# Attention over 16 images: the order of a batch's seven score products, and where the statistics and the input of the next batch stand

## The chip, the cores and the metric

The kernel runs on one core of one Trainium2 chip. The metric is the device time of one execution in microseconds (us), the median over several executions. A second, profiled execution gives the trace that the rows below are taken from; times in it are counted from the first instruction.

The engines are named as in the profile: PE is TensorE (matmuls), PEld its weight loads, DVE is VectorE, ACT is ScalarE, POOL is GpSimd, and SP is the engine that only issues transfers (DMAs). Each engine works through its own list of instructions in order. Where an instruction has to wait for another engine, everything behind it on the same engine waits as well.

## The reference

For each of 16 images `x` (512 channels, 32x32 = 1024 positions):

```python
h = group_norm(x, gn_w, gn_b)            # 32 groups of 16 channels
q, k, v = split(qkv_w @ h + qkv_b)       # three 512x512 products
attn = softmax((q^T k) / sqrt(512))      # 1024 x 1024
o = out_w @ (v attn^T) + out_b
return x + o
```

The softmax runs over the keys. Everything is float32, and the result must be float32-accurate.

## The kernel before

**Arithmetic.** The weights are multiplied together once, so that a batch has four steps on PE. T: `t = G h` with G the product of the weights of q and k. S: the scores, `t^T h`, 1024 keys by 1024 queries. V: `v = h^T U` with U the product of the weights of v and of the output. A: the output, `v` times the exponentials. Every float32 operand is kept as a rounded upper part (`_hi`, fp32r) and the rest (`_lo`), and each product is three matmuls, hi-hi, hi-lo and lo-hi (lines 459 to 461). ACT writes the upper parts; DVE writes the rests.

**Seven products in place of eight.** T, S and V (but for batch 0's T and V) are done as block products of Strassen's kind: seven products named A11, A12, S1, S2, S3, A22 and S4, each of a block of the one matrix, or a sum of blocks, with a block of h or a sum of blocks of h (`t1` to `t4`, written by `h_combined` and split by `h_combined_rest`, line 1289). The list `PRODUCTS` gives their order in the score step; T and V have lists of their own, which name the products.

**The score step on PE** (`score_products`). Each product has four units of six matmuls, one for each of four PSUM banks. A11 is opened in banks 0 to 3. ACT copies it to banks 4 to 7 (`copy_first`, line 869, semaphore `s_p1`), where A12 is added to it; ACT copies the sum to SBUF with the key bias (`copy_scores`, line 881): that is the first quarter of the scores (`s_c11`). In banks 0 to 3 the products S2, S3 and A22 are added one after the other, and between two of them ACT copies each bank out: after S2 (`s_p2`), after S3 (`s_p3`) and after A22 (`s_c21`, a quarter of the scores). S3's unit i waits for `s_p2` of bank i, and A22's unit i for `s_p3` of bank i. S1 is opened in banks 4 to 7 as soon as A12's sum has been copied out; DVE adds it to the copy made after S3 (`add_scores`, line 1438; `s_c22`). S4 is added on top of S1 once `s_c22` is there, and DVE adds that sum to the copy made after S2 (`s_c12`). The order before is A11, A12, S1, S2, S3, A22, S4.

**Half 0 and half 1.** Queries 0 to 511 are half 0, queries 512 to 1023 are half 1. Half 0's scores are `c11` and `c21`, half 1's are `c22` and `c12`. `max_step` (line 1450) keeps a running maximum of each half, POOL spreads it over the partitions (`max_all`, line 1165), `subtract_max` (line 1457) takes it off, and ACT does the exponential (line 900) and the upper part (line 915).

**The splits of t.** `t_sum_rest` (line 1431; line 1379 in batch 0) writes the rests of S1, S2, S3 and S4 in this order; between those of S2 and of S3 stand three `max_step`s of `c11`. Each counts `s_tlo` up. ACT, before its four copies after S2, waits until `s_tlo` is complete: `act.wait_ge(s_tlo, splits(b + 1))`.

**The statistics of the next batch.** x of batch b+1 is loaded into `xs`, the same tile that held x of batch b. ACT first adds the output bias to `xs` (`shift_input`, line 888), SP stores it to `out` (line 425), and then loads the next x (line 429). DVE then takes the statistics (`stats_part`, eight instructions, line 1230). `group_stats` on SP writes them to DRAM (line 370), waits until they have landed and reads them back with one group to a partition (line 378). After that DVE joins them (`group_variance`, lines 1562 and 1564), ACT takes the root (`group_std_part`, line 894) and does a small exponential behind it (line 895), so that the exponential's table is loaded again, and DVE forms the inverse (`group_root`), which SP spreads over the channels. ACT's instructions of a batch stand in one list, in which the four copies after S2 come before the four after S3, those before the four after A22, and those before `group_std_part`.

**The next T step.** T's third product, S2, needs `t2`, the second `h_combined_rest` of the batch. DVE does the first one (`t1`) before the four `scale_output`s (line 1547) of the output's half 1, and the others behind them. POOL loads the blocks of U that don't stay in SBUF (`load_u`, lines 1150 and 1152), four transfers of 1.5 MB together, once the score step's S2 is done.

Of the kernel before, what the change touches and what calls it, by code (L numbers as in the profile page):

```python
# [45 lines left out]
PRODUCTS = [(A11, "b11"), (A12, "b21"), (S1, "t1"), (S2, "t2"), (S3, "t3"), (A22, "t4"), (S4, "b22")]  # L46
P_A11, P_A12, P_S1, P_S2, P_S3, P_A22, P_S4 = range(7)
# [62 lines left out]
def attention_kernel(nc, x, wq, wk, wv, wo_t, cols, block_avg, out):  # L110
# [5 lines left out]
    with ctx:  # L116
# [228 lines left out]
        def _(sp):  # L345
# [69 lines left out]

            def store_u_s2():
# [4 lines left out]
            for b in range(B):  # L421
                for k in range(CT):
                    if b + 1 < B:
                        sp.wait_ge(s_shifted, b * CT + k + 1)
                        sp.dma_start(out_v[b, :, k, :], xs[:, k, :]).then_inc(s_sent[k], DMA)
                if b + 1 < B:
                    for k in range(CT):
                        sp.wait_ge(s_sent[k], (b + 1) * DMA)
                        sp.dma_start(xs[:, k, :], x_v[b + 1, :, k, :]).then_inc(s_x[k], DMA)
                    group_stats(b + 1)  # L430
# [315 lines left out]
        def _(act):  # L746
# [231 lines left out]
            for b in range(B):  # L978
# [29 lines left out]
                for k in range(CT):  # L1008
# [3 lines left out]
                    shift_input(b, k)  # L1012

                act.wait_ge(s_tlo, splits(b + 1))
                for i in range(CT):
                    copy_scores(b, P_S2, i, i, 8 + i, s_p2)
                if b == 0:
# [9 lines left out]
                if b + 1 < B:  # L1027
                    group_std_part(b + 1)
                if b == 0:
# [49 lines left out]
                if b + 1 < B:  # L1079
# [9 lines left out]
                    for c in range(CT):  # L1089
# [3 lines left out]
                        h_combined_part(b + 1, c)  # L1093

# [110 lines left out]
        def _(dve):  # L1205
# [403 lines left out]
            for b in range(B):  # L1609
# [57 lines left out]
                if more:  # L1667
                    for q in range(CT * NB):
                        stats_part(b + 1, q)
                if b == 0:  # L1670
                    for n, a in enumerate((S1, S2, S3, S4)):
                        g_sum_rest(a, n)
                if b == 1:
                    for n, a in enumerate((S1, S2, S3, S4)):
                        u_sum_rest(a, n)
                for i in range(CT):
# [3 lines left out]
                for i in range(CT):  # L1680
                    max_step(b, 0, CT + i, CT + i, s_c21, b * 4 + i + 1)
                if more:
                    group_variance(b + 1)
                for i in range(CT):
                    add_scores(b, P_S4, i, 8 + i, s_p2, s_c12)
                    max_step(b, 1, CT + i, i, s_c12, b * 4 + i + 1)

                for q in range(CT):
                    subtract_max(b, 0, q)
                if more:  # L1690
                    group_root(b + 1)
                    group_spread(b + 1)
                if b == 0:
# [6 lines left out]
                    if more:  # L1700
                        affine_pair(b + 1)
# [6 lines left out]
                else:  # L1708
# [16 lines left out]
                    if more:  # L1725
                        affine_pair(b + 1)
# [19 lines left out]
                if more:  # L1746
                    for k in range(CT):
                        key_dot(b + 1, k)
                    h_combined_rest(b + 1, 0)
                for c in range(CT if more else CT - 1):  # L1750
# [33 lines left out]
```

## Time and profile before

| | |
|---|---|
| three runs | 1984.97, 1984.98 and 1986.65 us, median 1984.98 |
| the profiled execution | 1984.35 us |
| its span, first to last instruction | 1982.6 us |
| PE busy | 1973.3 us |
| DVE busy | 1667.9 us (84% of the span) |
| ACT busy | 1123.0 us (57%) |
| POOL busy | 447.9 us (23%) |

The chain that ended last is made of PE for 91%. Busy times of an engine are those in which it had an instruction in hand; matmuls overlap, so the mean duration of one (389 ns for 512 columns) is more than the distance from one start to the next. The profiled execution's own time is 1.75 us more than its span, and 0.63 us under the median of the three runs.

In a timeline a row is: start, duration, engine, line, operation, what it writes and reads, how many of them; in brackets the idle time of the engine before it and what ended it.

### The profile page before, as it was taken

How to read it: one execution, taken by the hardware profiler on the slowest of the kernel's cores; microseconds unless marked ns; L12 is line 12 of the kernel's file. 1: busy time of each engine (PE TensorE's matmuls, PEld its weight loads, DVE VectorE, ACT ScalarE, POOL GpSimd, SP SyncE). 2: the span in 40 equal slices, each digit the busy share in tenths (PEclk: the TensorE clock that was granted, in tenths of full speed). 3: DMA queues.
4: the chain of work that ended last, by engine and by line, in shares of the span. 5: the costliest groups of instructions: out<-in, count | busy, mean ns of one | idle time of the engine just before them, and what ended most of it. 6: DMA issues, size and time to landing. Idle time of an engine off the chain costs nothing.

```text
span 1982.6 us, 26069 instructions
## 1 busy us (share of the span) xinstructions
PE 1973.3 (100%) x9895; PEld 1681.2 (85%) x9895; DVE 1667.9 (84%) x2010; ACT 1123.0 (57%) x1431; POOL 447.9 (23%) x306
## 2 busy tenths in 40 slices
PE   9999999999999999999999999999999999999999
PEld 7888878888888888888888888888888888888888
DVE  8897987969889798797988979788797988969866
ACT  6564636646465564645746466563664646556461
POOL 1112140121412213131131401214022141221311
PEclk9999999999999999999999999999999999999999
DMA  6305143051431604325033240424305143150411
GB/s 177 129 7 130 59 74 119 6 139 49 75 118 16 167 12 75 119 41 153 6 73 116 58 136 6 113 76 74 120 7 143 45 75 118 19 171 4 75 33 54
DMA packets 102636, 157.89 MB, mean 80 GB/s; under 512 B 49376, under 2 KB 51264, under 8 KB 102512
## 3 DMA queue, kind: packets, MB, share of 16 engines
q0 software_dynamic: 31264, 73.15, 17.0%
q1 hardware_dynamic: 71248, 83.08, 13.7%
q8 instruction: 79, 1.29, 0.3%
q14 instruction: 45, 0.37, 0.1%
HBM read 85.57 MB, written 68.26 MB: 78 GB/s over the span
## 4 chain that ended last, share of the span: by engine, by line
PE 91%; DVE 4%; DMA 2%; ACT 1%; issue 1%; POOL 1%; SPq 0%; DVEq 0%; POOLq 0%; ACTq 0%
PE ring L459 30%; PE ring L461 30%; PE ring L460 30%; DMA stage<-stage 1%; DVE r_lo L1289 1%; DMA out<-all_max 0%; DVE stage L1457 0%; POOL stage L1170 0%; DVE h_lo L1264 0%; DVE stage L1524 0%; ACT stage L761 0%; POOL out L1179 0%; DMA stage<-wq 0%; DVE stage L1373 0%; ACT stage L774 0%
## 5 line engine op out<-in xcount | busy, mean ns | idle before, releaser
L459 PE MATMUL ring<-r_hi 128*128 128x512 f32 (+1 forms) x1724 | 656.6, 381 | 0.2 <-DVE r_lo L1477 0.2
L460 PE MATMUL ring<-r_lo,r_hi 128*128 128x512 f32 (+1 forms) x1724 | 656.4, 381 | 0.0
L461 PE MATMUL ring<-r_hi,r_lo 128*128 128x512 f32 (+1 forms) x1724 | 656.2, 381 | 0.0
L459 PEld LDWEIGHTS ring<-r_hi 128*128 128x128 f32 x1724 | 324.2, 188 | 62.2 <-DVE r_lo L1477 0.7
L461 PEld LDWEIGHTS ring<-r_hi,r_lo 128*128 128x128 f32 x1724 | 324.2, 188 | 62.0
L460 PEld LDWEIGHTS ring<-r_lo,r_hi 128*128 128x128 f32 x1724 | 324.2, 188 | 61.4
L881 ACT ACTIVATE stage<-ring,keybias 128x512 f32<-128x512 f32 x256 | 175.2, 685 | 164.3 <-PE ring L461 161.6
L1170 POOL PARTITION_ALL_REDUCE stage<-stage x32 | 127.3, 3977 | 465.8 <-DVE stage L1530 465.8
L854 ACT ACTIVATE stage<-ring,by_tile 128x512 f32<-128x512 f32 x120 | 82.5, 688 | 250.7 <-PE ring L461 250.7
L1462 DVE TENSOR_TENSOR r_lo<-stage,r_hi 128x1024 fp32r<-128x1024 f32 x128 | 182.2, 1453 | 0.0
L1450 DVE TENSOR_TENSOR run_max<-run_max,stage 128x512 f32<-128x512 f32 x192 | 132.0, 694 | 54.1 <-ACT stage L881 49.3
L459 PE MATMUL ring<-h_hi,r_hi 128*128 128x512 f32 x444 | 172.8, 389 | 0.2 <-DVE r_lo L1379 0.2
L461 PE MATMUL ring<-h_hi,r_lo 128*128 128x512 f32 x444 | 172.7, 389 | 0.0
L460 PE MATMUL ring<-h_lo,r_hi 128*128 128x512 f32 x444 | 172.7, 389 | 0.0
L1457 DVE TENSOR_TENSOR stage<-stage,all_max 128x1024 f32<-128x1024 f32 x128 | 151.8, 1228 | 0.0
L900 ACT ACTIVATE stage<-stage 128x1024 f32<-128x1024 f32 x128 | 134.5, 1051 | 18.7 <-DVE stage L1457 18.7
L915 ACT ACTIVATE r_hi<-stage 128x1024 fp32r<-128x1024 f32 x128 | 135.8, 1061 | 2.9 <-PE ring L461 0.3
L1165 POOL PARTITION_ALL_REDUCE all_max<-run_max x32 | 57.9, 1810 | 304.6 <-DVE run_max L1450 160.2
L761 ACT ACTIVATE stage<-xs,by_tile 128x1024 f32<-128x1024 f32 x62 | 76.5, 1233 | 83.3 <-DMA sum_row<-stage 82.6
L1230 DVE BATCH_NORM_STATS2 stats<-xs 128x6 f32<-128x512 f32 x128 | 80.7, 684 | 47.3 <-DMA xs<-x_in 47.1
L1150 POOL DMA_DIRECT2D r_hi<-u_dram x15 | 8.5, 570 | 461.3 <-PE ring L461 461.3
L767 ACT ACTIVATE r_hi<-stage 128x1024 fp32r<-128x1024 f32 x64 | 68.0, 1063 | 76.1 <-DVE stage L1279 71.5
(199 smaller groups left out, 3979.2 us busy)
## 6 DMA issues: line engine op xcount, KB each, us to landing
xs<-x_in SPq DMA_DIRECT2D x64, 512.0 KB, 5.7
out<-xs SPq DMA_DIRECT2D x60, 512.0 KB, 2.7
out<-run_max POOLq DMA_DIRECT2D x60, 256.0 KB, 5.6
inv<-inv_row SPq DMA_DIRECT2D x32, 256.0 KB, 4.5
out<-spare POOLq DMA_DIRECT2D x30, 256.0 KB, 7.6
out<-all_max POOLq DMA_DIRECT2D x30, 256.0 KB, 5.0
r_hi<-g_dram POOLq DMA_DIRECT2D x15, 512.0 KB, 6.2
r_lo<-g_dram POOLq DMA_DIRECT2D x15, 512.0 KB, 5.5
```

Source lines behind the costliest of these rows:

```text
L459: nc.tensor.matmul(ps_out, st_hi, m_hi, start=first, stop=False, skip_group_check=goes_on)
L460: nc.tensor.matmul(ps_out, st_hi, m_lo, start=False, stop=False, skip_group_check=goes_on)
L461: return nc.tensor.matmul(ps_out, st_lo, m_hi, start=False, stop=last, skip_group_check=goes_on)
L854: nc.scalar.activation(stage[:, to + kk, :], ring[:, T_BANK[p] + kk, :], ACT.Identity, bias=t_bias[:, i:i + 1]).then_inc(done, 1)
L881: nc.scalar.activation(stage[:, to, :], ring[:, bank + i, :], ACT.Identity, bias=keybias[:, m:m + 1]).then_inc(done, 1)
L900: nc.scalar.activation(here, here, ACT.Exp, scale=SCALE).then_inc(s_exp, 1)
L915: nc.scalar.activation(p_pair(r_hi, b, nb, q), stage[:, 8 * nb + 2 * q:8 * nb + 2 * q + 2, :], ACT.Copy).then_inc(s_phi, 1)
L1170: nc.gpsimd.partition_all_reduce(stage[:, 8 * nb + 1, :], stage[:, 8 * nb, :], P, bass.bass_isa.ReduceOp.add).then_inc(s_allsum, 1)
L1230: nc.vector.bn_stats(stats[:, k, half, :], xs[:, k, half * HALF:(half + 1) * HALF]).then_inc(s_stats, 1)
L1450: nc.vector.tensor_tensor(run_max[nb][:, :], first, stage[:, 8 * nb + m, :], ALU.max).then_inc(s_rmax[nb], 1)
L1457: nc.vector.tensor_tensor(here, here, all_max[:, :].rearrange("p (o n) -> p o n", o=1).to_broadcast([P, 2, HALF]), ALU.subtract).then_inc( ...
L1462: nc.vector.tensor_tensor(p_pair(r_lo, b, nb, q), stage[:, 8 * nb + 2 * q:8 * nb + 2 * q + 2, :], p_pair(r_hi, b, nb, q).bitcast(FP32), AL ...
```

## The change

- `PRODUCTS` becomes A11, A12, S2, S3, A22, S1, S4. T's and V's orders stay, since their lists go by name.
- POOL's `load_u` waits for the score step's S2 by its number in the list, so it starts when the third product is done and not the fourth.
- ACT: from batch 1 on `group_std_part(b + 1)` stands right behind the four copies after S2, ahead of the four after S3 (in batch 0 it stays behind those after A22). `shift_input` stays between the copies of `c11` in batch 0 alone; for the later batches it stands at the end of the batch before, behind `h_combined_part`.
- SP: the stores of the shifted input, and the loads of the next, are a function, `change_input`. They stand at the same place in SP's list.
- DVE: from batch 1 on `group_variance`, `group_root` and `group_spread` stand right behind the eight `stats_part`s (in batch 1 with the splits of U's sums between them). Then come half 0's four last `max_step`s, then S1's four `add_scores` with their maxima, then S4's, with half 0's four `subtract_max`es between them in pairs. The second `h_combined_rest` moves ahead of the four `scale_output`s of half 1.

```diff
--- before.py
+++ after.py
@@ -43,8 +43,8 @@
 
 
 A22, S1, A11, S2, S3, A12, S4 = range(7)
-PRODUCTS = [(A11, "b11"), (A12, "b21"), (S1, "t1"), (S2, "t2"), (S3, "t3"), (A22, "t4"), (S4, "b22")]
-P_A11, P_A12, P_S1, P_S2, P_S3, P_A22, P_S4 = range(7)
+PRODUCTS = [(A11, "b11"), (A12, "b21"), (S2, "t2"), (S3, "t3"), (A22, "t4"), (S1, "t1"), (S4, "b22")]
+P_A11, P_A12, P_S2, P_S3, P_A22, P_S1, P_S4 = range(7)
 
 
 T_PRODUCTS = [P_A11, P_S1, P_S2, P_A12, P_S3, P_A22, P_S4]
@@ -413,20 +413,23 @@
                 for at, name in ((0, "a11"), (1, "a12")):
                     sp.dma_start(by_rows(u_dram[side, :, at, :]), u_raw(t, name).bitcast(FP32)).then_inc(s_u_out, DMA)
 
+            def change_input(b):
+
+                for k in range(CT):
+                    sp.wait_ge(s_shifted, b * CT + k + 1)
+                    sp.dma_start(out_v[b, :, k, :], xs[:, k, :]).then_inc(s_sent[k], DMA)
+                for k in range(CT):
+                    sp.wait_ge(s_sent[k], (b + 1) * DMA)
+                    sp.dma_start(xs[:, k, :], x_v[b + 1, :, k, :]).then_inc(s_x[k], DMA)
+
             def store_u_s2():
                 for n, (side, t) in enumerate(((0, r_hi), (1, r_lo))):
                     sp.wait_ge((s_uhi, s_ulo)[n], 2)
                     sp.dma_start(u_dram[side, :, 2, :], t[:, u_home(1, S2), :].bitcast(FP32)).then_inc(s_us2_out, DMA)
 
             for b in range(B):
-                for k in range(CT):
-                    if b + 1 < B:
-                        sp.wait_ge(s_shifted, b * CT + k + 1)
-                        sp.dma_start(out_v[b, :, k, :], xs[:, k, :]).then_inc(s_sent[k], DMA)
                 if b + 1 < B:
-                    for k in range(CT):
-                        sp.wait_ge(s_sent[k], (b + 1) * DMA)
-                        sp.dma_start(xs[:, k, :], x_v[b + 1, :, k, :]).then_inc(s_x[k], DMA)
+                    change_input(b)
                     group_stats(b + 1)
                 if b == 1:
                     store_u_s2()
@@ -1009,11 +1012,14 @@
                     if k == 0:
                         act.wait_ge(s_bias_out, (b + 1) * DMA)
                     copy_scores(b, P_A12, k, k, k, s_c11, CT)
-                    shift_input(b, k)
+                    if b == 0:
+                        shift_input(b, k)
 
                 act.wait_ge(s_tlo, splits(b + 1))
                 for i in range(CT):
                     copy_scores(b, P_S2, i, i, 8 + i, s_p2)
+                if 0 < b < B - 1:
+                    group_std_part(b + 1)
                 if b == 0:
                     for n, (a, count) in enumerate(((S1, 5), (S2, 6), (S3, 7), (S4, 8))):
                         g_sum_part(a, n, count)
@@ -1024,9 +1030,8 @@
                     copy_scores(b, P_S3, i, CT + i, 12 + i, s_p3)
                 for i in range(CT):
                     copy_scores(b, P_A22, i, CT + i, CT + i, s_c21)
-                if b + 1 < B:
+                if b == 0:
                     group_std_part(b + 1)
-                if b == 0:
                     exponential(b, 0, 0)
                     p_part(b, 0, 0)
                     exponential(b, 0, 1)
@@ -1091,6 +1096,8 @@
 
                             act.wait_ge(s_unit, unit(b, "A") + CT)
                         h_combined_part(b + 1, c)
+                    for k in range(CT):
+                        shift_input(b + 1, k)
 
         @block.gpsimd
         def _(pool):
@@ -1667,38 +1674,44 @@
                 if more:
                     for q in range(CT * NB):
                         stats_part(b + 1, q)
+                if b > 0 and more:
+                    group_variance(b + 1)
                 if b == 0:
                     for n, a in enumerate((S1, S2, S3, S4)):
                         g_sum_rest(a, n)
                 if b == 1:
                     for n, a in enumerate((S1, S2, S3, S4)):
                         u_sum_rest(a, n)
+                if b > 0 and more:
+                    group_root(b + 1)
+                    group_spread(b + 1)
+                for i in range(CT):
+                    max_step(b, 0, CT + i, CT + i, s_c21, b * 4 + i + 1)
+                if b == 0:
+                    group_variance(b + 1)
                 for i in range(CT):
                     add_scores(b, P_S1, i, 12 + i, s_p3, s_c22)
                     if i > 0:
                         max_step(b, 1, i, CT + i, s_c22, b * 4 + i + 1)
                 for i in range(CT):
-                    max_step(b, 0, CT + i, CT + i, s_c21, b * 4 + i + 1)
-                if more:
-                    group_variance(b + 1)
-                for i in range(CT):
+                    if i % 2 == 0:
+                        subtract_max(b, 0, i)
+                        subtract_max(b, 0, i + 1)
                     add_scores(b, P_S4, i, 8 + i, s_p2, s_c12)
                     max_step(b, 1, CT + i, i, s_c12, b * 4 + i + 1)
-
-                for q in range(CT):
-                    subtract_max(b, 0, q)
-                if more:
+                if b > 0 and more:
+                    affine_pair(b + 1)
+
+                if b == 0:
                     group_root(b + 1)
                     group_spread(b + 1)
-                if b == 0:
                     for q in range(CT):
                         p_rest(b, 0, q)
                         first_v_rest(q)
                     first_v_rest(4)
                     subtract_max(b, 1, 0)
                     subtract_max(b, 1, 1)
-                    if more:
-                        affine_pair(b + 1)
+                    affine_pair(b + 1)
                     first_v_rest(5)
                     sum_tree(b, 0)
                     first_v_rest(6)
@@ -1722,8 +1735,6 @@
                     subtract_max(b, 1, 0)
                     add_v12(b, 1)
                     subtract_max(b, 1, 1)
-                    if more:
-                        affine_pair(b + 1)
                     v12_rest(b, 0)
                     v12_rest(b, 1)
                     subtract_max(b, 1, 2)
@@ -1747,6 +1758,7 @@
                     for k in range(CT):
                         key_dot(b + 1, k)
                     h_combined_rest(b + 1, 0)
+                    h_combined_rest(b + 1, 1)
                 for c in range(CT if more else CT - 1):
                     scale_output(b, 1, c)
                     if not more:
@@ -1755,7 +1767,7 @@
                     last_scale(0)
                     last_scale(1)
                 if more:
-                    for c in range(1, CT):
+                    for c in range(2, CT):
                         h_combined_rest(b + 1, c)
```

## Rows read from the trace of the kernel before

**Rows 1.** The page, part 1: busy time, share of the span, instructions.

```profile
PE 1973.3 (100%) x9895; PEld 1681.2 (85%) x9895; DVE 1667.9 (84%) x2010; ACT 1123.0 (57%) x1431; POOL 447.9 (23%) x306
```

**Rows 2.** PE's waits: line, waited for, us in total, times, longest.

```profile
PE ring L459 <- DVE r_lo L1289: 3.0, 2, 2.0
```

**Rows 3.** Start of batch 2's T step: timelines of DVE and PE; a window with PEclk.

```profile
285.80 5.24 DVE L1289 TENSOR_TENSOR r_lo<-stage,r_hi 128x1024 fp32r<-128x1024 f32 x3
...
288.82 0.50 PE L459 MATMUL ring<-r_hi,g_hi 128*128 128x512 f32 x1 [1.98 <-DVE r_lo L1289]
...
290.10:293.40 3.30, 3.30 (x9) 2.61 (x8) 0.94 (x1) 0.72 (x2) 1.78 (x2) 0.50 0.92 86
```

**Rows 4.** Timeline of PE, score step of batch 5: starts of products 1, 3, 5.

```profile
666.93 0.39 PE L459 MATMUL ring<-h_hi,r_hi 128*128 128x512 f32 x1
...
677.81 0.39 PE L459 MATMUL ring<-r_hi 128*128 128x512 f32 x1
...
688.69 0.39 PE L459 MATMUL ring<-r_hi 128*128 128x512 f32 x1
```

**Rows 5.** Timeline of ACT, score step of batch 5.

```profile
684.89 0.69 ACT L881 ACTIVATE stage<-ring,keybias 128x512 f32<-128x512 f32 x1 [3.04 <-PE ring L461]
...
700.53 1.28 ACT L894 ACT_TABLE_LOAD   x1
702.37 0.20 ACT L894 ACTIVATE by_group<-by_group 32x1 f32<-32x1 f32 x1 [0.55 <-DVE by_group L1564]
...
703.88 0.20 ACT L895 ACTIVATE by_group<-by_tile 32x1 f32<-32x1 f32 x1
```

**Rows 6.** Timeline of DVE, score step of batch 5.

```profile
680.84 0.69 DVE L1450 TENSOR_TENSOR run_max<-run_max,stage 128x512 f32<-128x512 f32 x1 [0.92 <-ACT stage L881]
681.45 2.36 DVE L1431 TENSOR_TENSOR r_lo<-stage,r_hi 128x1024 fp32r<-128x1024 f32 x2
686.77 5.13 DVE L1230 BATCH_NORM_STATS2 stats<-xs 128x6 f32<-128x512 f32 x8 [2.97 <-DMA xs<-x_in]
...
701.16 1.00 DVE L1562 BATCH_NORM_AGGREGATE by_group<-inv 32x2 f32<-32x192 f32 x1
702.19 0.14 DVE L1564 TENSOR_SCALAR by_group<-by_group 32x1 f32<-32x1 f32 x1
```

**Rows 7.** Timelines of SP and POOL, batch 5; then lines 370 and 378, 15 each.

```profile
691.94 0.38 SPq L370 DMA_DIRECT2D stats_d<-stats  x1
697.39 0.32 SPq L378 DMA_DIRECT2D inv<-stats_d  x1
...
689.17 0.57 POOL L1150 DMA_DIRECT2D r_hi<-u_dram  x1 [30.61 <-PE ring L461]
...
DMA to landing us min/median/max: 2.2/4.5/5.5
...
DMA to landing us min/median/max: 1.5/1.7/2.8
```

**Rows 8.** Timeline of PE, the first matmuls of all, and six like them later.

```profile
1.45 4.02 PE L504 MATMUL ring<-spare 128*128 128x512 bf16 x9 [1.45 <-DVE spare L1206]
...
17.05 1.47 PE L504 MATMUL ring<-spare 128*128 128x512 bf16 x6
```

**Rows 9.** Timeline of DVE, batch 1: U's sums and the statistics.

```profile
195.20 2.50 DVE L1506 TENSOR_TENSOR stage<-u_hi,u_lo 128x512 f32<-128x512 f32 x4
...
200.40 4.84 DVE L1230 BATCH_NORM_STATS2 stats<-xs 128x6 f32<-128x512 f32 x8
```

**Rows 10.** Timelines of PE and DVE, score step of batch 0.

```profile
72.21 0.39 PE L459 MATMUL ring<-r_hi 128*128 128x512 f32 x1
...
71.47 1.29 DVE L1379 TENSOR_TENSOR r_lo<-stage,r_hi 128x512 fp32r<-128x512 f32 x2
...
77.39 0.69 DVE L1395 TENSOR_TENSOR stage<-stage,spare 128x512 f32<-128x512 f32 x1
...
84.55 0.69 DVE L1399 TENSOR_TENSOR r_lo<-stage,r_hi 128x512 fp32r<-128x512 f32 x1
```

## The prediction, made before the changed kernel was run

> **What bounds the kernel now.** The page first: PE is busy in 1973.3 of 1982.6 us, no other engine over 84% [rows 1]. So only what makes PE wait can change the time, and nearly nothing is left to be won: the reader should take from this that a gain can be a few us, while a new wait of PE counts in full. Then PE's waits: the only ones of size are for line 1289, `h_combined_rest`, 3.0 us in two [rows 2]. The timeline of DVE and PE shows why: the second `h_combined_rest` stands behind the four `scale_output`s and starts at 285.80, and PE, which needs `t2`, starts again at 288.82 after 1.98 us of idleness. From 290.1 to 293.4 PE then runs at a granted clock of 0.50, 1.2 GHz in place of 2.4 [rows 3]. Last the score step of batch 5, which stands for batches 2 to 14: I need who hands what to whom, and when. PE starts the step at 666.93 and spends 10.88 us on two products, so 5.44 on one and 1.36 on a unit; it does not wait [rows 4]. What follows counts from 666.93 as S+0.
>
> **The second `h_combined_rest`, moved up.** It then ends about 1.2 us after the first and before `t2` is wanted; the four scales behind it slip by 1.2 us, and PE's S1 of the T step, which needs the first two, comes 2.7 us into that step. So the waits of rows 2 go (3.0), the stretch at half clock too (3.3 us at 0.50, 1.65 lost) [rows 3], and a few tenths of restarts: -5.0.
>
> **The input shifted and loaded early.** ACT's four shifts leave the score step and go where ACT idles before the T step; the x transfers land during T. DVE's 2.97 us of idleness for x goes [rows 6], but DVE is not the bound, so by itself 0. It moves one thing: the last maximum of `c11` waited for ACT, which was held up by the shifts. The copy can start 0.28 us after PE's unit, as it does at 684.89, 0.28 after a unit that ended at 683.25 + 1.36 [rows 4, 5]. A12 ends at 677.81, so the copy runs from 678.09 to 678.78 and the maximum starts at 678.81 and not at 680.84 [rows 4, 6]. The rests behind it move by the same 2.03: S4's ends at 681.78 (S+14.85).
>
> **The new order and the copies after S2.** S3 is now due at S+16.32. Its first unit needs the first copy after S2, and ACT makes it only when the rest of S4 is there: S+14.85 + 0.69 = S+15.54. It is 0.8 us in time, from batch 1 on: 0. If that margin is gone, PE waits here and the row will name ACT.
>
> **`group_std_part` ahead of the copies after S3: the large term.** A22 is now due at S+21.76 (688.69) [rows 4], and its first unit needs the first copy after S3. ACT makes that copy only when it is through with `group_std_part`, which waits for `group_variance` on DVE, which waits for a round trip through DRAM, which starts when all eight statistics are done; and these still stand behind S4's rest. Step by step:
> - statistics: DVE is free at 681.78. Eight took 4.84 us where x was there [rows 9], so they end at 686.6. That x is there early helps no more than that, since DVE's list holds them back.
> - the round trip: out, landed, back, landed. The medians are 4.5 and 1.7 us [rows 7], so 6.2. The loads of U lie beside it in the trace: they began 2.8 us before the store (689.17, 691.94) [rows 7]. `load_u` now starts a product earlier, at about 683.7, and the store at 686.6: 2.9 us, the same company, so I take the medians. Back at 692.8.
> - `group_variance`: from 701.16 to 702.33, 1.17 us [rows 6]. 694.0.
> - ACT: root, table load, small exponential, from 702.33 to 704.08, 1.75 us [rows 5] (the table load ahead of the root runs before the wait, at 700.53, and is hidden). 695.7.
> - the copy: 0.69 [rows 5]. 696.4, and PE starts A22 at about 696.5.
>
> Due 688.69, started 696.5: PE idles 7.8 us. Queued behind the waiting `group_std_part` are all of ACT's copies; who waits for them is PE, and behind PE every other engine. A restart costs 0.1 (0.50 for the first matmul [rows 3] in place of 0.39 [rows 4]). After the stall the clock will be down, since 1.98 us of idleness brought it down [rows 3]. The two ends for that: 1.65 us as there, and what the start of the program shows, when PE had done nothing before: nine matmuls took 4.02 us, where at full clock six take 1.47, so nine 2.1, and the two products behind them ran at the lower level as well; with these some 5.3 us at 1.2 GHz, 2.6 lost [rows 8]. An idleness of 7.8 us is nearer to the second: 2.6. A batch then costs 7.8 + 0.1 + 2.6 = 10.5, and 13 batches (2 to 14; the last has no next one) 136.5.
>
> A rule of the skill bears on the round trip. The Trainium skill (DMA: Bandwidth & Descriptors, Anatomy of one DMA) puts a fixed 2.0 us on each transfer, most of it the receipt of the write; two small transfers would be 4.0 us and the sum 2106. The trace has 4.5 and 1.7, and agrees with the rule only at its low end (2.2, 1.5) [rows 7].
>
> **Batch 1** has U's sums between S4's rest and the statistics: 5.2 us (195.20 to 200.40) [rows 9]. Its u loads are over by then, so I take the shortest round trip, 3.7 [rows 7]. S+14.85 + 5.2 + 4.84 + 3.7 + 1.17 + 1.75 = S+31.5; then ACT has four upper parts of U's sums before the copy (put at 2.5, as DVE's four [rows 9]) and 0.69: S+34.7. PE idles 12.9; with 0.1 and 2.6 that is 15.6.
>
> **Batch 0** keeps the old place of `group_std_part`, but not the old order. S3 is due at 72.21, where the fourth product starts now; S4's rest ends at 71.47 + 1.29, the copy 0.69 later, at 73.5 [rows 10]: 1.3. A22's first unit waits for ACT, which first splits G's sums: the last sum is there at 78.1 [rows 10], plus two instructions of at most 0.69 gives 79.4, due 79.05: 0.35. S4's first unit needs `c22`, now behind four maxima (0.69 and a hand-over, 0.8 each), `group_variance` and one addition; the copies of `c21` can't start before 85.24 [rows 10], so 85.9 + 3.2 + 1.2 + 0.7 = 91.0, due 90.4: 0.6. With restarts 2.6 in all.
>
> **Half 0's maxima first, the subtractions in pairs.** In the S4 product DVE now has eight short instructions and four subtractions of 1.2 us, 10 us against PE's 5.44, so `c12` comes late; but V asks for it only at its fifth product, 11 us into V. Covered: 0. `group_root` and `group_spread` leave the V step, and DVE gets slack there that PE can't use: 0.
>
> **The sum.** Against the profiled execution: 1984.35 + 136.5 + 15.6 + 2.6 - 5.0 = 2134.1. The median of the runs stands 0.6 above that execution, so 2135.
>
> **The ends.** Shortest round trip, 3.7, and 1.65 for the clock: 5.3 + 0.1 + 1.65 = 7.05 a batch, 91.7 for 13, batch 1 14.7, in all 2089. Longest round trip, 8.3 (5.5 + 2.8) [rows 7]: 9.9 + 0.1 + 2.6 = 12.6, 164 for 13, batch 1 20, and half clock in batch 0 too (1.65), with only 3 won back: 2170.
>
> **Rivals.**
> 1. *The wait never reaches PE* (not slower). Its place is `group_std_part` on ACT; its price is nothing if the variance is there by S+19.3 (21.76 less 0.69 and 1.75), which with 6.2 and 1.17 before it needs the statistics done by S+11.9. For it: x lands early, and DVE has idle gaps in just that stretch (0.92 us and more before each maximum) [rows 6]. Against it: the statistics stand behind the rests in DVE's list, which end at S+14.85, and nothing takes them forward. It would give 1984.98 - 5.0 + 2.6 = 1982.6, within 0.2%, or a little less if batch 0 loses nothing. 6%.
> 2. *The short round trip.* If the earlier loads of U leave the two small transfers alone, they take 3.7, a batch 8.0, and the time is 2102. For it: batch 1 and the minima of rows 7; against it: the same 2.8 us between the loads and the store as before. The skill's fixed cost, cited above, says nearly the same. 11%.
> 3. *The clock stays down.* If after such a stall PE stayed at 1.2 GHz to the end of the step, the 16.3 us left of it would cost 16.3 and not 2.6: 14 x 13.7 more, 2327. Rows 3 and 8 speak against it: the clock came back after 3.3 and 5.3 us of work. 3%.
>
> My forecast has the other 80%. That the change does less than it says I can't see: PE's first unit of A22 waits for `s_p3` whatever the order.
>
> **How the numbers follow.** About 0.2%, 4 us, is what a measurement of this kernel can tell from no change. Range 2089 to 2170: the forecast with both its ends, and rival 2. Rival 1 lies within 0.2% or just over it; I give 4% to no change and 2% to faster; the rest, 94%, is slower.
>
> **What would show each step.** In PE's waits a new row: `ring L459 <- ACT stage L881` (or what stands before it), 14 long ones of 6 to 10 us, batch 1's about 13. On ACT an idle time of 6 us or more before the root (line 894), ended by DVE's line 1564, and on DVE one before line 1562, ended by the DMA `inv<-stats_d`. PEclk at 0.5 in a stretch after each. No waits for line 1289. Line 1230 without idleness for x. In batch 0 three waits of 0.3 to 1.4 us. Wrong would be: a PE without idle stretches at A22 in batches 2 to 14; a `group_variance` that ends before S+19.3; or stalls at another product, S3 or S4, in the later batches.

## The result, and the profile after

The changed kernel takes 2129.43 us (median of 4 runs, 2128.04 to 2129.98), the kernel before 1985.74 us on the same chip: a ratio of 1.0724, 95% interval 1.0708 to 1.074. It is 144 us slower; the prediction said 2135, 2089 to 2170. The profiled execution has a span of 2128.2 us, 145.6 more than before.

From the page after, part 1, the answer to [rows 1], and from PE's waits, the answer to [rows 2]:

```profile
PE 2003.4 (94%) x9894; PEld 1701.0 (80%) x9895; DVE 1668.5 (78%) x2010; ACT 1114.6 (52%) x1431; POOL 448.5 (21%) x306
...
PE ring L462 <- ACT stage L884: 118.8, 15, 13.1
```

The reader is to see two things. DVE, ACT and POOL are busy for as long as before, within 9 us, with as many instructions: no work was added. PE's share of the span has fallen from 100% to 94%, though its busy time is 30 us longer: the matmuls behind each stall run at the lower clock, as shown below. And one row of waits holds 118.8 of the 145.6 us: line 462 is the hi-hi matmul, line 884 the copy of the scores out of PSUM. The row for `h_combined_rest` is gone.

Batch 5 after, timelines of PE (the first matmul of A22), ACT, DVE, SP and POOL; the score step starts at 711.02, the S+0 of the prediction. They answer to [rows 4 to 7]:

```profile
741.37 0.77 PE L462 MATMUL ring<-r_hi 128*128 128x512 f32 x1 [8.43 <-ACT stage L884]
...
725.88 2.42 ACT L884 ACTIVATE stage<-ring,keybias 128x512 f32<-128x512 f32 x4 [3.03 <-DVE r_lo L1438]
728.32 1.28 ACT L897 ACT_TABLE_LOAD   x1
738.93 0.20 ACT L897 ACTIVATE by_group<-by_group 32x1 f32<-32x1 f32 x1 [9.33 <-DVE by_group L1571]
739.15 1.28 ACT L898 ACT_TABLE_LOAD   x1
740.45 0.20 ACT L898 ACTIVATE by_group<-by_tile 32x1 f32<-32x1 f32 x1
740.56 2.37 ACT L884 ACTIVATE stage<-ring,keybias 128x512 f32<-128x512 f32 x4
...
723.49 2.35 DVE L1438 TENSOR_TENSOR r_lo<-stage,r_hi 128x1024 fp32r<-128x1024 f32 x2
725.76 4.84 DVE L1237 BATCH_NORM_STATS2 stats<-xs 128x6 f32<-128x512 f32 x8
737.72 1.01 DVE L1569 BATCH_NORM_AGGREGATE by_group<-inv 32x2 f32<-32x192 f32 x1 [7.12 <-DMA inv<-stats_d]
...
730.62 0.38 SPq L370 DMA_DIRECT2D stats_d<-stats  x1
735.81 0.33 SPq L378 DMA_DIRECT2D inv<-stats_d  x1
...
727.82 0.57 POOL L1157 DMA_DIRECT2D r_hi<-u_dram  x1 [24.73 <-PE ring L464]
```

Read from the bottom up, this is the chain. The loads of U start at 727.82. The statistics end at 730.60, SP stores them at once, and the store takes until 735.8; the read back takes until 737.7. DVE sits idle for 7.12 us, ACT for 9.33 us with the table for the root already loaded, and behind this wait in ACT's list stand the copies after S3, for which PE waits 8.43 us. The two transfers, 15 each, with the time to landing (lines 370 and 378, the same two rows as in [rows 7]):

```profile
DMA to landing us min/median/max: 2.6/4.8/5.5
...
DMA to landing us min/median/max: 1.5/1.7/1.9
```

The clock after a stall, windows of batch 4 (PE idle, then working at the low clock, then at the full one) and of batch 5; the last three numbers are PEclk, DMA share, GB/s:

```profile
605.00:609.00 4.00, 0.00 (x0) 0.00 (x0) 1.99 (x8) 2.25 (x5) 0.00 (x0) 0.50 0.01 2
609.20:614.80 5.60, 5.60 (x13) 4.39 (x14) 0.69 (x1) 2.29 (x5) 0.00 (x0) 0.50 0.06 4
615.00:620.00 5.00, 5.00 (x24) 4.13 (x23) 2.72 (x4) 1.78 (x3) 0.72 (x1) 1.00 0.01 2
...
737.90:744.50 6.60, 3.13 (x8) 2.50 (x9) 1.81 (x8) 4.10 (x8) 0.00 (x0) 0.50 0.05 1
```

The clock is down to 1.2 GHz while PE is idle, and PE then works at it for 5.7 us in batch 4, 13 matmuls in 5.6 us where 24 fit in 5.0 at 2.4 GHz, and for 3.3 us in batch 5.

### The profile page after: what moved, and what is told of

Same layout as the page of the kernel before. It is cut to its first block, busy times and chain, and to the rows that moved or that the text cites. A ratio compares the mean times of both kernels' runs of the same rounds, so it can differ in the third digit from the quotient of the medians.

```text
span 2128.2 us, 26068 instructions
## 1 busy us (share of the span) xinstructions
PE 2003.4 (94%) x9894; PEld 1701.0 (80%) x9895; DVE 1668.5 (78%) x2010; ACT 1114.6 (52%) x1431; POOL 448.5 (21%) x306
## 4 chain that ended last, share of the span: by engine, by line
PE 86%; DVE 7%; DMA 4%; ACT 2%; issue 1%; ACTq 0%; DVEq 0%
PE ring L462 28%; PE ring L463 28%; PE ring L464 28%; DVE stats L1237 3%; DMA stats_d<-stats 3%; DVE r_lo L1438 1%; DMA inv<-stats_d 1%; ACT stage L884 1%; ACT L898 1%; DVE by_group L1569 1%; DVE run_max L1457 1%; PE ring L485 0%; PE ring L478 0%; PE ring L487 0%; PE ring L507 0%
## 5 line engine op out<-in xcount | busy, mean ns | idle before, releaser
L462 PE MATMUL ring<-r_hi 128*128 128x512 f32 (+1 forms) x1724 | 670.8, 389 | 118.9 <-ACT stage L884 118.8
L463 PE MATMUL ring<-r_lo,r_hi 128*128 128x512 f32 (+1 forms) x1724 | 667.7, 387 | 0.0
L464 PE MATMUL ring<-r_hi,r_lo 128*128 128x512 f32 (+1 forms) x1724 | 666.6, 387 | 0.0
L462 PEld LDWEIGHTS ring<-r_hi 128*128 128x128 f32 x1724 | 331.9, 193 | 188.8 <-issue 123.5
L464 PEld LDWEIGHTS ring<-r_hi,r_lo 128*128 128x128 f32 x1724 | 330.9, 192 | 65.0
L463 PEld LDWEIGHTS ring<-r_lo,r_hi 128*128 128x128 f32 x1724 | 331.9, 192 | 63.2
L884 ACT ACTIVATE stage<-ring,keybias 128x512 f32<-128x512 f32 x256 | 162.9, 681 | 131.0 <-PE ring L464 81.1
L1413 DVE TENSOR_TENSOR stage<-stage,ring 128x512 f32<-128x512 f32 x90 | 60.6, 686 | 79.0 <-PE ring L464 68.8
L935 ACT ACTIVATE ring<-ring 128x512 f32<-128x512 f32 x30 | 17.5, 582 | 186.3 <-PE ring L464 186.3
```

The lines of the kernel that those rows point to most:

```text
L462: nc.tensor.matmul(ps_out, st_hi, m_hi, start=first, stop=False, skip_group_check=goes_on)
L463: nc.tensor.matmul(ps_out, st_hi, m_lo, start=False, stop=False, skip_group_check=goes_on)
L464: return nc.tensor.matmul(ps_out, st_lo, m_hi, start=False, stop=last, skip_group_check=goes_on)
L884: nc.scalar.activation(stage[:, to, :], ring[:, bank + i, :], ACT.Identity, bias=keybias[:, m:m + 1]).then_inc(done, 1)
```

## The experiments

**The place of `group_std_part`, taken back on ACT alone.** From the changed kernel:

```diff
-                if 0 < b < B - 1:
-                    group_std_part(b + 1)
...
-                if b == 0:
+                if b + 1 < B:
                     group_std_part(b + 1)
```

> The changed kernel with one edit: group_std_part goes back behind ACT's four copies after A22. Theory (the copies after S3 wait behind group_std_part for the statistics' round trip): the 14 long waits of PE at A22 (8.2 us each) go. But DVE keeps group_root ahead of half 0's last maxima, and it now waits for ACT's root, which comes after the last copy after A22, at S+29.7 (S is the start of the score step). Then 2.0 us of group_root and group_spread, four maxima 2.9, one addition 0.7: c22 at S+35.2, where S4 is due at S+32.64. So PE waits 2.6 us at S4 in 14 batches, with restart and half clock some 4.5 each: 1980 + 63 = 2043 us. Rival (the new order itself, or the early x, costs PE its time, not the place of group_std_part): the long waits stay at A22, about 2129.

Measured: 2014.69 us, ratio 1.0156 (1.0135 to 1.0176). The long waits at A22 are gone, so the rival falls. In their place stand 1.58 us at S4 in each of batches 2 to 14, and 8.3 in batch 1. DVE, batch 2, and PE:

```profile
342.77 0.15 DVE L1576 RECIPROCAL by_group<-by_group 32x1 f32<-32x1 f32 x1 [2.35 <-ACT by_group L897]
342.95 0.21 DVE L1578 SCALAR_TENSOR_TENSOR by_group<-by_group 32x1 f32<-32x1 f32 x1
...
343.63 3.08 DVE L1456 TENSOR_TENSOR run_max<-run_max,stage 128x512 f32<-128x512 f32 x4
346.63 1.28 DVE L1444 TENSOR_TENSOR stage<-stage,ring 128x512 f32<-128x512 f32 x2
...
347.45 0.47 PE L462 MATMUL ring<-h_hi,r_hi 128*128 128x512 f32 x1 [1.58 <-DVE stage L1444]
```

The mechanism is as expected: root on ACT, `group_root`, four maxima, one addition, PE. The size was not: 2015 us, where I had 2043. `group_root` and `group_spread` took 0.9 us (342.77 to 343.7) and not 2.0, and 1.58 us of idleness did not bring the clock down in any of the 13 batches, so a batch lost 1.8 us and not 4.5. Batch 1 lost 10.6 us, far more than I had allowed. ACT's timeline of batch 1 shows why:

```profile
214.01 2.42 ACT L884 ACTIVATE stage<-ring,keybias 128x512 f32<-128x512 f32 x4 [9.20 <-DVE u_lo L1524]
```

These are the copies after A22. They wait for the splits of U's sums, which stand behind the variance on DVE, and the root stands behind the copies.

**The place of the statistics' steps, put into the kernel before.** The order of the products, x and t2 stay:

```diff
                     copy_scores(b, P_S2, i, i, 8 + i, s_p2)
+                if 0 < b < B - 1:
+                    group_std_part(b + 1)
...
+                if b > 0 and more:
+                    group_variance(b + 1)
...
```

(both are taken from their old places)

> The kernel before with one part of the change: from batch 1 on group_variance stands right behind the statistics and group_std_part ahead of the copies after S3; the order of the products, x and t2 stay as before. Theory: the place of group_std_part alone is enough. The statistics end at S+25.2 (they wait for x), 6.3 for the round trip, 1.2, 1.75 and the copy 0.7 give S+35.3, where A22 is due at S+27.2 in the old order: 8.1 idle, with restart and clock 10.4, 13 times 135, batch 1 about 12: 2132 us. Rival (the stall needs the new order, in which A22 comes a product earlier): no long waits, 1985 us.

Measured: 2124.05 us, ratio 1.0707 (1.0686 to 1.0728). PE's waits:

```profile
PE ring L459 <- ACT stage L881: 112.4, 14, 9.4
```

Fourteen waits of 7.5 to 9.4 us in the kernel before, from this edit alone. The sum had said 2132, 8 us too much; the waits of 13 batches are 7.9 us in the mean, as forecast within 0.2, and part of the rest is that the stretch at half clock for `t2` did not come in this execution. The move is enough, and the new order is not needed for it: A22 comes a product earlier in the changed kernel, but so do the statistics, and the two cancel.

**The loads of U held back.** In the changed kernel:

```diff
                 pool.wait_ge(s_unit, unit(b, "S") + 4 * P_S2 + 4)
+                if 1 < b < B - 1:
+                    pool.wait_ge(s_gstep, b * GSTEP + 2)
```

> The changed kernel, with POOL's loads of U held back in batches 2 to 14 until group_variance is done. Theory (the first half of the round trip is long, 4.9 us, because 1.5 MB of U move beside it): the store lands in 2.3 to 2.7 us as in batches 0 and 1, PE's idle time at A22 falls from 8.2 to about 5.8 us, 13 x 2.4 = 31 less: 2098 us. Rival (the transfer is slow for itself, or by something else such as the number of its small packets): it still takes 4.9 us, 2129 us. V needs U only 13 us later, so no new wait at V in either case.

Measured: 2099.82 us, ratio 1.0585 (1.0564 to 1.0606), 30 us less than the changed kernel. Time to landing of the store of the statistics, and PE's waits:

```profile
DMA to landing us min/median/max: 2.1/2.4/3.0
...
PE ring L462 <- ACT stage L884: 86.4, 15, 12.6
```

The store fell from 4.8 to 2.4 us and PE's waits by 32.4 us, 2.5 in each of the 13 batches. The 24 KB of the statistics are slow because 1.5 MB of U are on their way. What is left, 2.4 + 1.7, is the round trip alone. The Trainium skill (DMA: Bandwidth & Descriptors, Anatomy of one DMA) gives a fixed 2.0 us for a transfer that GpSimd issues; these two go out from SP, and each half is close to it all the same. The same page (Latency and other measured facts) puts HBM's latency at 0.2 us on average and at 2 us at high load; the 2.4 us that the loads of U add point the same way, but no run here separates that latency from the queues.

**The statistics moved forward.** The changed kernel, with the condition of the first rival made true:

```diff
                     t_sum_rest(b, S2)
+                    if more:
+                        for q in range(CT * NB):
+                            stats_part(b + 1, q)
+                    t_sum_rest(b, S3)
+                    t_sum_rest(b, S4)
                     for i in range(1, CT):
                         max_step(b, 0, i, i, s_c11, b * 4 + i + 1)
-                    t_sum_rest(b, S3)
-                    t_sum_rest(b, S4)
+                    if more:
+                        group_variance(b + 1)
```

> The changed kernel with the statistics of the next x moved forward on DVE, ahead of the rests of S3 and S4, and the three c11 maxima and group_variance behind those. This makes the condition of the prediction's first rival true: x is there at about S+7.5, the statistics run from S+8.5 to S+13.3, before the loads of U start, so the round trip is 4.3, the variance is done at S+18.9 and ACT has made the first copy after S3 at S+21.5, due S+21.76. Theory: the long waits of batches 2 to 14 vanish or shrink below 0.5 us, and a wait of 0.1 to 0.3 us at S3 appears, since S4's rest ends at S+15.7 and the copy at S+16.4, due S+16.3. Batch 1 keeps about 5 us (U's sums come behind the variance, and ACT splits them before the copies). 1985 - 7.3 + 2.6 + 7 + 15 x 0.3 = about 1992 us. Rival (PE's wait comes from something else in ACT's list, such as the table loads): waits of several us stay, over 2050.

Measured: 1986.81 us, ratio to before 1.0017 (1.0007 to 1.0027). Timelines of DVE and ACT, batch 5, whose score step starts at 670.38, and PE's waits:

```profile
678.70 4.84 DVE L1237 BATCH_NORM_STATS2 stats<-xs 128x6 f32<-128x512 f32 x8
...
688.06 1.01 DVE L1569 BATCH_NORM_AGGREGATE by_group<-inv 32x2 f32<-32x192 f32 x1
...
685.83 2.42 ACT L884 ACTIVATE stage<-ring,keybias 128x512 f32<-128x512 f32 x4 [3.63 <-DVE r_lo L1438]
688.27 1.28 ACT L897 ACT_TABLE_LOAD   x1
689.57 0.20 ACT L897 ACTIVATE by_group<-by_group 32x1 f32<-32x1 f32 x1
...
PE ring L462 <- ACT stage L884: 4.9, 2, 3.6
```

`group_std_part` stands where the change put it, table loads and all, and ACT no longer waits in it, since the variance (done at 689.2) is there before the table is. Apart from the start, PE waits only in batches 0 and 1. So it is neither the two table loads nor the place as such: it is when the variance arrives, which the end of the statistics (S+19.6 in the changed kernel, S+13.2 here) and the round trip behind it (6.6 and 4.3 us) set together. The time is 5 us less than worked out: the waits of 0.1 to 0.3 us at S3 that I expected did not come, since the copy started at S+15.45, and batch 1 waited 3.6 us and not 5.

**Everything but the statistics' steps.** The changed kernel with `group_std_part`, `group_variance`, `group_root`, `group_spread` and `affine_pair` at their old places:

```diff
-                if b > 0 and more:
-                    group_variance(b + 1)
...
-                if b > 0 and more:
-                    group_root(b + 1)
-                    group_spread(b + 1)
                 for i in range(CT):
                     max_step(b, 0, CT + i, CT + i, s_c21, b * 4 + i + 1)
-                if b == 0:
+                if more:
                     group_variance(b + 1)
...
```

> The changed kernel with the next batch's statistics back at their old places on both engines: group_std_part behind the copies after A22, group_variance behind half 0's last maxima, group_root, group_spread and affine_pair as in the kernel before. The new order of the products, the early x and the moved second h_combined_rest stay. Theory (the statistics' place is all that costs): no long waits of PE are left. Of the waits of before, those for line 1289 go (6 us with the stretch at half clock), batch 0's 2.6 us come: 3 to 5 us faster than before, ratio 0.9975 to 0.9985. Rival (the new order or the early x costs time too, hidden so far under the stalls): same or slower than before.

Measured: 1980.04 us, ratio 0.9974 (0.9964 to 0.9984): 4.7 us faster than before, as worked out. The only wait over 1 us behind the start is batch 0's:

```profile
PE ring L462 <- ACT stage L884: 1.3, 1, 1.3
```

No wait of the later batches is left, so neither the order nor x costs anything there in this company, and the 149 us between this and the changed kernel are the statistics' steps.

**The second `h_combined_rest` alone**, in the kernel before:

```diff
                     h_combined_rest(b + 1, 0)
+                    h_combined_rest(b + 1, 1)
...
-                    for c in range(1, CT):
+                    for c in range(2, CT):
```

> The kernel before with one part of the change: the second h_combined_rest ahead of the four scale_outputs of half 1. Theory: PE's waits for line 1289 and the stretch at half clock go, nothing else changes: 5 to 6 us faster, ratio about 0.997. Rival (the scales, now 1.2 us later, become the wait: the T step's S1 opens their banks): a wait for line 1547 in place of the other, time the same.

Measured: 1978.38 us, ratio 0.9966 (0.9953 to 0.9978). No wait for line 1289 and none for the scales is left; the moved instruction is worth 6 us, nearly all that there is to win. It is also 1.7 us less than the version above, which has this move, the new order and the early x: no run shows a gain from the new order. The 12 executions of the kernel before beside this one lie between 1982.6 and 1988.6 us, the longest with a mean granted clock of 0.998 and the shortest with 1.000, while the five of this version lie within 0.6 us, all at 1.000. So the stretch at half clock in [rows 3] seems to come in some executions more often than in others, and the move takes it away; that is read from the clocks' means, since only one execution has a trace.

**The early x alone**, in the kernel before:

```diff
-                    shift_input(b, k)
+                    if b == 0:
+                        shift_input(b, k)
...
+                    for k in range(CT):
+                        shift_input(b + 1, k)
```

> The kernel before with one part of the change: from batch 1 on ACT shifts x at the end of the batch before, so that x of the next batch is loaded during the T step. Theory: DVE's 3 us of idleness for x goes and S4's rest ends at S+14.85 in place of S+16.9, but PE waits for neither, so the time stays within 1 us of before. Rival (x's 4 MB in the T step hold up the additions to the output, and with them the scales and the second h_combined_rest): more or longer waits for line 1289, up to 5 us slower; or the other way, that the x transfers leave the score step free and make it a few us faster.

Measured: 1981.13 us, ratio 0.9987 (0.9978 to 0.9996). A small miss: it is 2 us faster, where I had it within 1. The trace has two waits for `h_combined_rest` still, but of 1.0 us at most, and no stretch at half clock:

```profile
PE ring L459 <- DVE r_lo L1292: 1.6, 2, 1.0
```

All 11 executions had a mean granted clock of 1.000, where those of the kernel before on the same chip had 0.999 or 1.000. Why the waits are shorter is open.

**The new order alone**, in the kernel before, the statistics' steps at their old places:

```diff
-PRODUCTS = [(A11, "b11"), (A12, "b21"), (S1, "t1"), (S2, "t2"), (S3, "t3"), (A22, "t4"), (S4, "b22")]
+PRODUCTS = [(A11, "b11"), (A12, "b21"), (S2, "t2"), (S3, "t3"), (A22, "t4"), (S1, "t1"), (S4, "b22")]
...
```

(the list of places behind it, and DVE's maxima and subtractions, are changed as in the change itself)

> The kernel before with the new order of the products and of DVE's maxima and subtractions alone; x, t2 and the statistics as before. Theory (the 0.8 us margin of the first copy after S2 comes from the early x): ACT's shifts hold the last copy of c11 up, S4's rest ends at S+16.9 and the copy at S+17.6, where S3 is due at S+16.3: PE waits 1.25 us in each of batches 1 to 15, with the restart 20 us in all, and no half clock since 1.2 us of idleness did not bring it. With batch 0's 2.6: 2007 us. Rival (the margin is not tied to x): 2.6 us slower than before, no row of waits at S3.

Measured: 2013.30 us, ratio 1.0142 (1.0128 to 1.0156). PE's waits:

```profile
PE ring L462 <- ACT stage L884: 20.8, 17, 1.4
PE ring L462 <- DVE r_lo L1292: 2.8, 3, 1.7
PE ring L462 <- DVE stage L1441: 2.4, 4, 1.0
```

The first row is the wait at S3, 1.26 us in 14 of batches 1 to 15 (1.42 in batch 2), as worked out, with batch 0's 1.26 and one of 0.46 in batch 1. The time is 6 us over the sum of 2007. The second row, the waits for `t2` (line 1292), was in the time before and stays. The third was not in my sum but for batch 0's: with x late, the variance comes late too and holds up S1's additions (line 1441). And a wait and its restart cost 1.5 us, not 1.3. So of the three parts the order is the one that costs, 29 us, and the early x is what pays for it.

**A version that beats both.** The one with the statistics' steps at their old places, and batch 0 mended:

```diff
                     for kk in range(2):
                         first_sum_rest(S4, kk)
+                    for i in range(1, CT):
+                        max_step(b, 0, i, i, s_c11, b * 4 + i + 1)
...
+                if b == 0:
+                    for n, a in enumerate((S1, S2, S3, S4)):
+                        g_sum_rest(a, n)
                 if more:
                     for q in range(CT * NB):
                         stats_part(b + 1, q)
```

(the maxima and the splits are taken from their old places, and batch 0's `group_variance` goes behind S1's additions)

> As the previous one with the statistics at their old places, and with batch 0 mended: the rests of S3 and S4 ahead of the three c11 maxima, the splits of G's sums ahead of the statistics, group_variance behind S1's additions. Theory: batch 0's three waits (1.3, 0.35 and 0.55 us and restarts) go, which is 2.0 to 2.6 us less than the kernel with the statistics put back, and 6 to 7 us less than before: ratio 0.9965 to 0.997. Rival (batch 0's new order makes other waits, at G's sums or at V): not faster than the one without.

Measured: 1977.36 us, ratio 0.996 (0.9946 to 0.9973), 2.7 us less than without the mended batch 0 and 7.4 less than before, a little more than forecast. Of PE's waits over 0.1 us only those of the start are left:

```profile
PE ring L507 <- DVE spare L1212: 1.5, 1, 1.5
PE ring L485 <- DVE r_lo L1222: 0.8, 1, 0.8
PE ring L462 <- DVE r_lo L1385: 0.3, 1, 0.3
```

## Why the prediction was right

By its own steps; measured values are of the profiled execution, batches 2 to 14 unless another is named:

| step | predicted | measured |
|---|---|---|
| statistics end (batch 5) | S+19.6 | S+19.6 (730.60) |
| round trip | 6.2 | 6.6 (4.94 + 1.70, means of 13) |
| variance, root, table load, exponential | 2.9 | 1.2 and 1.75 |
| PE idle at A22 | 7.8 | 8.0 |
| restart and clock | 2.7 | 2.4 |
| 13 batches | 136.5 | 135.5 |
| batch 1 | 15.6 | 14.8 |
| batch 0 | 2.6 | 2.5 |
| won back | -5.0 | -7.2 |

The idle time of a batch is the 118.8 us of the waits' row less batch 0's 1.26 and batch 1's 13.1, over 13. Restart and clock is the rest of what a stall cost: what the starts of the matmuls across it and behind it lie apart over their usual 0.227 us, less the idle time. The profile counts idleness from the modelled end of the last matmul, 0.16 us after the next one was due, so this 0.16 us is in that row. The last row is what remains of the 145.6 us.

- The large term stood on one reading of ACT's list, the root ahead of the copies that PE waits for, and on DVE's list, which holds the statistics back although x is there. The experiments agree from both sides: the edit alone makes the stall in the kernel before, and taking the root's wait away, by moving the root back or by having its input there in time, takes the stall away.
- The round trip was 0.4 us short, and a batch idled 8.0 and not 7.8. That I took the slow medians, since the loads of U keep their distance of 2.8 us to the store, was right, and the held-back loads show that they are the cause. Rival 2, the short round trip, is nearly what that experiment made (4.1 and not 3.7): 2100, where it had said 2102.
- The clock was the weaker term. I took 2.6 from the start of the program, the nearer of two rows; it came to between 1.4 and 3.0 us from batch to batch, 2.2 in the mean, though the idleness was nearly the same. The bounds of 1.65 and 2.6 were passed on both sides. That 13 batches came out at 135.5 against 136.5, closer than either term, is partly luck: the longer idleness and the shorter loss by the clock offset each other. Batch 1 is alike: its round trip took 4.4 us and not 3.7, its idleness 13.1 and not 12.9, and the clock cost it 1.5 and not 2.6.
- Batch 0's sum is right by offsetting too: its waits were 1.26, 0.11 and 0.39 us, where I had 1.3, 0.35 and 0.6, and each restart cost 0.24 us, not 0.1.
- The clock stayed down for no longer than 6.2 us of work (batch 10), so rival 3 falls. Rival 1, no stall at all, needed the statistics to be done by S+11.9. With DVE's list changed they were done at S+13.2, the round trip was 4.3 since in batch 5 the loads of U began at 687.18, when the store had landed (686.2), and the stall was gone: its point of decision held once the 1.9 us of shorter round trip are counted.
- Won back was the term most off, 2.2 us too small, and the largest part of why the kernel is 6 us faster than the 2135. The sum counted the two waits of the waits' view and the clock. The trace has smaller ones that I didn't count: in the T steps of batches 5, 6 and 12, of 0.1 to 0.4 us with their restarts, and two of batch 1, in V and at the start of A, of 0.6 us each with theirs, which the changed kernel hasn't either. They come to about 1.9 us.
- The margin of the first copy after S2, 0.8 us, held in every batch, and the experiment with the order alone shows what it is worth: without the early x it becomes a wait of 1.26 us in each batch.

## What to carry to other kernels

Where an engine that copies results out for the bound engine takes up an instruction that waits for something far away, everything behind it in its list waits too: before moving such an instruction forward, work out when its last input is there, the whole way through DRAM included, and not only when the engine would have a gap. A small transfer that others depend on can be slowed by megabytes that are sent off just before it (here from 2.4 to 4.8 us); either hold those back or start the small one first. And a part of a change can be needed by another part (x by the order) while the third one, here a single moved instruction, brings nearly the whole gain, 6.3 of 7.4 us.

## What the runs showed of the hardware that I had not expected

**DVE beside a POOL reduction.** In the kernel before, the multiply-and-multiply of `group_root` took 1.04 us, in the changed kernel 0.21, with the same 32 numbers. In the first it starts together with a `PARTITION_ALL_REDUCE` on POOL. Before (DVE, POOL):

```profile
712.30 1.04 DVE L1572 SCALAR_TENSOR_TENSOR by_group<-by_group 32x1 f32<-32x1 f32 x1
...
712.30 1.78 POOL L1165 PARTITION_ALL_REDUCE all_max<-run_max  x1 [9.06 <-DVE stage L1457]
```

After, the third `h_combined_rest` has taken the place of the second beside the long reduction (DVE, POOL, batch 5), and with it the long duration: the first of the two takes 3.11 us of the 4.25, the other 1.22:

```profile
694.38 4.25 DVE L1296 TENSOR_TENSOR r_lo<-stage,r_hi 128x1024 fp32r<-128x1024 f32 x2
...
691.93 6.07 POOL L1135 PARTITION_ALL_REDUCE stage<-stage  x1
```

So the wait for `t2` in [rows 3] was partly this: 285.80 to 288.77 is 2.97 us for an instruction that takes 1.22 elsewhere, and a reduction ran on POOL until 289.27. The trace bears it out beyond these rows: in the kernel before 47 of DVE's instructions took over 0.4 us more than the median of their kind (same line, operation and shape), in the changed kernel 47 again, and each of them lay beside a `PARTITION_ALL_REDUCE`. `group_root` is not among the 47, since all 15 of its multiplications were slow. Not every one that lay beside one was slow (298 did in the kernel before), and what they read parts them: the 45 subtractions of 128x1024 from two SBUF tiles (`h_combined_rest` and the like) that lay beside a reduction for nine tenths of their time or more took 1.8 to 3.3 us, most of them 3.2, in place of 1.2, while the 45 operations of 128x512 there with one operand in PSUM (`ring`) took 0.69 us, as elsewhere. No run took the reduction away, so what in it does this is open.

**The clock and the length of an idleness.** Behind the start, idle times of PE up to 1.7 us never brought the clock down (13 of 1.58 us in one kernel, 1.26 us in each batch of another); one of 1.98 us, one of 3.6 and all of over 5 us did. Behind idle times of 5.1 to 6.1 us (loads of U held back) and of 7.5 to 8.6 us PE lost the same, 1.4 to 3.0 us: what was lost did not grow with the idleness. In the changed kernel the work at the low clock behind a stall lasted 5.2 to 6.2 us in six of the batches 2 to 14 and 2.8 to 4.1 us in the other seven, in turn up to batch 11. The Trainium skill (TensorE: Matmul & The Clock Gate, What's actually happening) says that the point at which the clock changes depends on where, in a rhythm that runs by itself, the first matmul falls, and gives a variation of 0.5 us to either side; the alternation from batch to batch agrees with the rhythm, the spread here is larger.
